# Ternary weights made on GpSimd alone, partly inside a self attention loop; a norm root moved; expert rows numbered by lane

## The reference, cut to what matters

```python
x = x + wkv(layernorm(x), ctx)                 # stage 0, a recurrence as scans
x = x + self_attention(layernorm(x))           # stage 1: 16 heads, one shared key/value per token,
                                               #          picked by the argmax of a gate
x = x + cross_attention(layernorm(x), ctx)     # stage 2: int8-rounded norm and weights
x = x + f8_matmul(layernorm(x))                # stage 3
x = x + channel_attention(layernorm(x), ctx)   # stage 4: softmax over channels, 128 units
x = x + ternary_ffn(layernorm(x))              # stage 5: weights as below
x = x + batch_attention(layernorm(x), ctx)     # stage 6
x = x + experts(layernorm(x))                  # stage 7: top 2 of 8 experts per token

def ternary_quant(w_fp32, g=64):
    w = w_fp32.astype(bfloat16); w_g = w.reshape(-1, g)
    scale = clip(mean(abs(w_g), -1), 1e-8, None)
    q = clip(round(w_g / scale), -1, 1)
    return w + ((q * scale).reshape(w.shape) - w)
```

## Time and profile before

| what | value |
|---|---|
| median of 3 runs | 828.03 us (826.43 to 833.64) |
| profiled execution, its own time | 824.63 us |
| its span, first to last instruction | 822.9 us |
| mean granted TensorE clock | 0.892 of full |
| busy: TensorE matmul, VectorE, ScalarE, GpSimd | 636.2, 502.4, 288.2, 247.4 us |

### The profile page before, as it was taken

One profiled execution on the slowest core, in us unless ns is written; L12 is line 12 of the kernel. 1 busy time (PEld: TensorE's weight loads), 2 busy tenths in 40 slices (PEclk: granted clock), 3 DMA queues, 4 the chain that ended last, 5 costly groups with the idle time before them and its releaser, 6 DMA issues.

```text
span 822.9 us, 10939 instructions
## 1 busy us (share of the span) xinstructions
PE 636.2 (77%) x3677; PEld 400.8 (49%) x3678; DVE 502.4 (61%) x1083; ACT 288.2 (35%) x519; POOL 247.4 (30%) x247
## 2 busy tenths in 40 slices
PE   1632888885972278889878999843999999999991
PEld 1331335443662124555544667531566666666661
DVE  6998986875988899999666445853222222222223
ACT  4810432324567005767843234501122111111210
POOL 3212243546821297644221015001111111111110
PEclk9885998997996559999979999955999999999996
DMA  7002302020005433561310003994000000000004
GB/s 256 0 0 55 112 1 65 14 52 0 2 1 104 98 83 96 139 167 52 92 39 1 0 1 150 430 427 143 20 26 26 25 25 25 25 25 25 19 14 166
DMA packets 34140, 61.83 MB, mean 75 GB/s; under 512 B 6232, under 2 KB 29784, under 8 KB 31768
## 3 DMA queue, kind: packets, MB, share of 16 engines
q1 hardware_dynamic: 24992, 48.93, 18.7%
q10 hardware_dynamic: 6896, 6.29, 2.3%
q0 software_dynamic: 2208, 6.03, 2.3%
HBM read 47.35 MB, written 13.50 MB: 74 GB/s over the span
## 4 chain that ended last, share of the span: by engine, by line
PE 47%; DVE 22%; DMA 3%; issue 3%; ACT 1%; POOL 1%; DVEq 0%; SPq 0%; POOLq 0%; ACTq 0%
PE bank L1820 17%; PE bank L1841 8%; DVE region L1191 4%; PE bank L1429 4%; PE bank L1450 3%; PE bank L1114 2%; DMA norm_rows<-XN 2%; PE bank L1831 2%; PE bank L1074 2%; PE bank L1098 2%; DVE XN L357 1%; DVE wide L1178 1%; PE bank L1955 1%; DVE region L1264 1%; DVE region L756 1%
## 5 line engine op out<-in xcount | busy, mean ns | idle before, releaser
L1820 PE MATMUL bank<-region,wide 128*128 x368 | 143.6, 544 | 0.3 <-issue 0.3
L1720 DVE TENSOR_TENSOR wide<-wide,bank 128x448 f32<-128x448 f32 x46 | 28.6, 621 | 127.3 <-ACT wide L1764 127.3
L1820 PEld LDWEIGHTS bank<-region,wide 128*128 128x128 f32 x368 | 68.8, 192 | 61.3 <-issue 61.1
L1191 DVE TENSOR_REDUCE region<-bank 128x2 f32<-128x512 f32 x128 | 80.3, 679 | 3.5 <-PE bank L1074 3.1
L1137 ACT ACTIVATE region<-bank 128x1024 f32<-128x1024 f32 x64 | 63.1, 1025 | 47.8 <-PE bank L1098 47.7
L1626 POOL DMA_INDIRECT choice_results<-wide,to_row x23 | 22.7, 987 | 181.6 <-DVE wide L1733 181.6
L1841 PE MATMUL bank<-region,XN 128*128 x322 | 73.4, 380 | 1.2 <-DVE wide L1733 1.2
L1074 PE MATMUL bank<-region 128*128 128x256 bf16 x256 | 53.2, 308 | 19.1 <-DVE region L1191 15.1
L1764 ACT ACTIVATE wide<-bank 128x448 f32<-128x448 f32 x46 | 25.0, 543 | 111.8 <-PE bank L1820 111.8
L1841 PEld LDWEIGHTS bank<-region,XN 128*128 128x128 f32 x322 | 59.6, 190 | 9.2 <-issue 2.1
L371 POOL TENSOR_TENSOR rstd<-vareps,half_neg 128x4 f32<-128x4 f32 x16 | 17.3, 1084 | 120.0 <-DVE vareps L367 119.8
(11 more groups left out here) (304 smaller groups left out, 1229.5 us busy)
## 6 DMA issues: line engine op xcount, KB each, us to landing
region<-in_L_ffn_experts_dram SPq DMA_DIRECT2D x8, 2688.0 KB, 24.0
region<-ctx_parts SPq DMA_DIRECT2D x24, 192.0 KB
region<-norm_parts SPq DMA_DIRECT2D x24, 192.0 KB
channel_values<-wide ACTq DMA_DIRECT2D x8, 512.0 KB, 4.4
ctx_parts<-region SPq DMA_DIRECT2D x40, 64.0 KB, 2.1
region<-in_L_ffn_w_gate_up_dram SPq DMA_DIRECT2D x4, 512.0 KB, 6.4
wide<-channel_values SPq DMA_DIRECT2D x16, 128.0 KB, 2.5
norm_parts<-region SPq DMA_DIRECT2D x24, 64.0 KB, 3.2
```

The lines of the kernel that those rows point to most:

```text
L1191: e.tensor_reduce(nmax[i % 2][:, at_:at_ + KC], score_bank("scores", n).rearrange("p (c n) -> p c n", c=KC), AX.X, ALU.max, negate=True).t ...
L1720: e.tensor_tensor(HB8[par][:, cols], silu8[:, cols], bank[hf][:, 512:512 + I8 // 2], ALU.mult)\
L1820: last = e.matmul(bank[hf][:, 512 * gu:512 * gu + hw], xbT[par][:, P * c:P * c + P], region[:, bass.ds(off + (2 * gu + c) * I8 + hw * hf, ...
```

## The change

1. VectorE's two compares per chunk are gone. GpSimd makes each chunk with six instructions: the quotient by the scale (to f32), two clamp-and-round steps (`tensor_scalar` with two operations each), times the scale, minus w, plus w. VectorE's closing step of the sums makes a reciprocal instead of two thresholds.
2. Nine of the 36 instructions run in the self attention loop, behind the context part of turns 2 to 8 (1, 1, 1, 2, 2, 1, 1 of them). The other 27 run in one row after GpSimd's splits of the norm in the channel attention, with no semaphore between them and VectorE.
3. At the start of the cross attention, the key blocks of tiles 0 and 1 and the norm root come ahead of the value bias of tiles 0 and 1.
4. The token row number becomes 8 * lane + tile. The norm rows are stored in two halves, each as soon as its half of the norm is there, with 4 KB pieces; results come back with 2 KB pieces. One VectorE instruction of the row search becomes two of half the width.

```diff
-        tscale, tlow, thigh = beside(TG), beside(TG), beside(TG)
+        tscale, tinv = beside(TG), beside(TG)
+        tsign = beside(1024, BF16)
+        EARLY6 = 9
...
@@ pool_attention, s == 0, turn t >= 1
                         for p in ((0,), (1, 2), (3,), (4,), (5,), (6, 7), (8,), (9,))[t - 1]:
                             pool_context_part(e, ch, p // 5, p % 5)
+                        if t == 2:
+                            e.wait_ge(s_tern["weights_summed"], 1)
+                        for p in ((), (0,), (1,), (2,), (3, 4), (5, 6), (7,), (8,))[t - 1]:
+                            pool_ternary_op(e, ch, p // 6, p % 6, traw[0])
@@ pool_attention, s == 1
+                for i in range(2):
+                    kbd(i)
+                pool_norm(e, 2, 4, NT)
+                e.wait_ge(s_att["norm_quantised"], NT)
                 for i in range(NT):
-                    kbd(i)
+                    if i >= 2:
+                        kbd(i)
                     e.tensor_tensor(V[:, i, :], V[:, i, :], bvrow, ALU.add).then_inc(s_att["v_ready"], 1)
                     e.wait_ge(s_att["v_ready"], i + 1)
-                    if i == 1:
-                        pool_norm(e, 2, 4, NT)
-                        e.wait_ge(s_att["norm_quantised"], NT)
@@ pool_channel_tiles
-            for c in range(TW // TCH):
-                pool_ternary_weights(e, ch, c)
+            for step in range(6 * TW // TCH):
+                if step // 6 * 6 + step % 6 >= EARLY6:
+                    pool_ternary_op(e, ch, step // 6, step % 6, f8a)
@@ vec_channel
-            pair_steps([(maxima, 0), (maxima_parts, 1), (weights, 0)])
+            pair_steps([(maxima, 0), (maxima_parts, 1)])
@@ vec_ternary_sums, last chunk
-                e.tensor_scalar(thigh, tscb, 0.5 + 2.0 ** -9, None, ALU.mult)
-                ch.link(e.tensor_scalar(tlow, tscb, -(0.5 + 2.0 ** -9), None, ALU.mult))
+                ch.link(e.reciprocal(tinv, tscb))
+                e.tensor_scalar(tinv, tinv, 0.5 / (0.5 + 2.0 ** -9), None, ALU.mult).then_inc(s_tern["weights_summed"], 1)
+        def pool_ternary_op(e, ch, c, step, tquot):
...
+                ch.link(e.tensor_tensor(by_group(tquot), by_group(w), spread(tinv[:, g]), ALU.mult))
+                ch.link(e.tensor_scalar(tquot, tquot, 1.0, MAGIC, ALU.min, ALU.add))
+                ch.link(e.tensor_scalar(tsign, tquot, MAGIC - 1.0, MAGIC, ALU.max, ALU.subtract))
+                ch.link(e.tensor_tensor(by_group(tsign), by_group(tsign), spread(tscb[:, g]), ALU.mult))
+                ch.link(e.tensor_tensor(tsign, tsign, w, ALU.subtract))
+                ch.link(e.tensor_tensor(w, w, tsign, ALU.add))
@@ results_in
-                            ys_dram[N * k + 2 * P * j:N * k + 2 * P * (j + 1), :].rearrange("(t p) d -> p t d", p=P))\
+                            ys_dram[N * k:N * k + N, :].rearrange("(p t) d -> p t d", t=NT)[:, 2 * j:2 * j + 2, :])\
@@ vec_experts
-            ch.link(e.tensor_scalar(hi_hot[:, :, 0, :], hi_hot[:, :, 0, :], lane_1, None, ALU.mult))
+            for k in range(2):
+                last = e.tensor_scalar(hi_hot[:, NT * k:NT * k + NT, 0, :], hi_hot[:, NT * k:NT * k + NT, 0, :],
+                                       lane_rows[:, k:k + 1], None, ALU.mult)
+            ch.link(last)
@@ act_experts
-            leave_half(XT8, 0, 6, s_turn, s_turned, base=TURN["moe"])
-            leave_half(XT8, 1, 0, s_turn, s_turned, base=TURN["moe"])
+            for hf in range(2):
+                e.wait_ge(s_xn, 7 * NT + 4 * (hf + 1))
+                e.dma_start(xn_dram.rearrange("(p t) d -> p t d", t=NT)[:, 4 * hf:4 * hf + 4, :],
+                            XN[:, 4 * D * hf:4 * D * hf + 4 * D].rearrange("p (t d) -> p t d", d=D))\
+                    .then_inc(s_moe["norm_stored"], 16)
+                leave_half(XT8, hf, (6, 0)[hf], s_turn, s_turned, base=TURN["moe"])
...
-            e.wait_ge(s_xn, 8 * NT)
-            e.dma_start(xn_dram.rearrange("(t p) d -> p t d", p=P), XN[:, :].rearrange("p (t d) -> p t d", d=D))\
-                .then_inc(s_moe["norm_stored"], 16)
```

42 lines of the change are left out of this document (14 added, 28 removed).

## The result

The kernel after took 822.32 us (median of 20 runs, 818.81 to 827.14), the kernel before 827.39 us (20 runs, 824.69 to 833.64). The ratio is 0.9936, 95% interval 0.992 to 0.9952: 5.1 us faster by the medians, about half of what was forecast, and within 1%. The two profiled executions have spans of 820.4 (after) and 822.9 us (before) and granted clocks of 0.884 and 0.892.

A forecast was written before the change was run, and what follows sets the result against it. VectorE was taken as the bound, busiest in the channel attention with TensorE close behind. Terms +0.1 + 6.2 - 1.6 - 11.5 - 2.8 - 0.3 = -9.9 us took 828.0 to 818.1 us, range 810.5 to 826.5.

The forecast's parts named there:

- channel attention: Compares leave VectorE, TensorE narrowly becomes the bound, last maxima end at 382.1 against 393.64: -11.5 us (-15 to -7).
- nine instructions in the loop: Self attention loop: GpSimd's added instructions delay key blocks and VectorE's select, +6.2 us (+3 to +11).
- norm root first: Start of cross attention: two bias additions leave GpSimd's list ahead of the norm root, -1.6 us (-1.8 to 0).
- store of the norm rows: Start of the experts: halves land by about 550, so `from_row` sets off the first fetch, -2.8 us (-2.9 to 0).
- results' return: End of the experts: 2 KB pieces may shorten the return of the results, -0.3 us (0 to -0.8).
- The rival that named it: GpSimd's `tensor_scalar` takes 2.13 or more; turns 3, 7 and 8 bring 2 to 4 us more: 821 us, chance 0.1.
- turns 7 and 8, +0.2: Self attention loop: each adds 1.04 us on GpSimd, last key blocks late by -0.5 to +1.0: +0.2 us.
- turn 3, put at 0: Self attention loop: adds 1.04 us on GpSimd, but the scores it feeds start later than GpSimd is done: 0.
- a rival with 0.07: Self attention loop: longer key-block waits drop TensorE's clock in five more turns, +15.8 on the sum, 834 us; chance 0.07.
- The steps by position: Self attention loop, costs worked along GpSimd's order: turn 2 +1.8, turns 3 and 4 0, turn 5 +1.15, turn 6 +3.0 us.
- The rival of late maxima: Channel attention stays bound by maxima queued behind operand loads; gain 6 in place of 11.5, 823.6 us; chance 0.15.
- 49 us, 57 at the upper bound: Channel attention: GpSimd's 27 late instructions run from 302 to 351 to 359, hidden, as TensorE wants the weights after 380.

The follow-up runs named there:

- before_rows: The kernel before with only the experts' part of the change (row numbering, halved norm-row store, 2 KB result pieces): 824.86 us, ratio 0.9957.
- nine_int16: The kernel after, early instructions kept in the loop, rounding by three (mult, add) `tensor_scalar` instead of two of 3.64 us: 816.84 us, ratio 0.9899.
- all_late: The kernel after with all 36 GpSimd instructions in the late row of the channel attention, none in the self attention loop: 823.77 us, ratio 0.9946.
- before_root_first: The kernel before with only the norm root of stage 2's second half moved ahead of the second value bias add: 827.33 us, ratio 1.001.
- late_int16: The kernel after with all ternary instructions late, clamp and round by three (mult, add) `tensor_scalar` through int16: 808.48 us; repeat 810.15 us.

## Why the prediction was right or wrong

By the time it was right in direction and range: 822.3 in 810.5 to 826.5. Its 818.1 lay 4.2 us too low: 9.9 us of gain were forecast and 5.1 measured. The range is 16 us wide, so lying in it says little, and the outcome that the prediction held likeliest, over 1% faster at 0.59, didn't come; within 1% had 0.36. It is also in part luck: the loop cost 6.7 us more than its term and the channel attention gave 2.6 more than its own, which partly cancel. (The range's lower end, worked out as the text says, is 818.1 - 3.2 - 2.5 = 812.4, not near 811.) Term by term, with what the traces gave; they add up to the 2.5 us between the two spans, not to the 5.1 of the medians:

| term | forecast | trace |
|---|---|---|
| closing step of the sums | +0.1 | at most +1.3 by the second key repeat; before_rows, without it, had +1.0 |
| nine instructions in the loop | +6.2 (+3 to +11) | +12.9 |
| norm root first | -1.6 | -1.7 local |
| channel attention | -11.5 (-7 to -15) | -14.1 |
| store of the norm rows | -2.8 | -3.4 |
| first expert block | none | +1.6, by the clock |
| results' return | -0.3 (-0.8 to 0) | +0.6 |

- **What failed is the sum of the loop**, +6.2 against +12.9, in two places of it. The first is the size "I take 1.04, since it reads one input as the cast does". The number of inputs doesn't set this price, the operations do: 3.64 us. It shows in "turns 7 and 8, +0.2", the tail: +5.1. The rival that named it had stopped at 2.13 and some 2 to 4 us. Removing it from the loop is worth 4.1 us in the profile (181.3 to 177.2) and 5.5 by the medians of after and nine_int16, though these were not run side by side.
- The second is turn 3, put at 0 and measured at 2.7: TensorE's longer wait in turn 2 and the clock behind it. I priced the waits as waits and kept the clock for a rival with 0.07, arguing from L524 at 0.39 behind a wait of 1.80. Behind 3.81 it was 0.61 and the clock 0.50. This rival happened in part: turns 2, 3 and 6 and the tail ran at 0.84 to 0.91 in the mean. It wasn't the five more turns that I priced at 15.8, so it didn't end slower than before. The Trainium skill, page TensorE: Matmul & The Clock Gate, Part 1, was cited for this, and the trace agrees with it: the throttled state is where TensorE falls back to. It doesn't account for all falls here: in turn 4 of the kernel before the clock was 0.73 in the mean, and in that turn and the one before it TensorE never stood longer than 1.4 us.
- **The steps by position held, and the contention with them.** The waits of 3 to 4 us at the scores of tiles 2 and 6 came as 3.81 and 4.57. Turn 2 cost 1.3 of 1.8, turn 5 1.2 of 1.15, turn 6 2.6 of 3.0, each by VectorE's select held up beside GpSimd's products, as the prediction says of L731. In turn 2 it is right in size by another way than its own: it reasoned from the delay of the key blocks, which TensorE pays in turn 3. Turn 4 cost 0, as forecast. With the fast form the loop cost 6.7 to 8.4, near the forecast 6.2, but partly by another cause, the clock.
- **The channel attention went as described**: TensorE became the bound at 2.85 us per two pairs. Its term was 2.6 us too small, mostly because six microseconds at half clock were allowed for the double work, which cost 3.0 us. The double work began at 314.20 and the clock was full from 315.8 on (0.78 in the mean from 314 to 318), so 1.6 us at half speed cost 0.8. The rival of late maxima can be laid aside: VectorE idled 4.4 us in all.
- "49 us, 57 at the upper bound" for the late row was 69.5: it began at 312.6, as the whole stage came 12 us later, and ended at 382.1. In all_late TensorE wanted the weights at 396.90 - 11.79 = 385.1, 3.9 us behind the last maxima; by the same distance it wants them at 395.7 in the kernel after. So the cover of over 20 us was 13.6, and nine instructions more would have used it up.
- **Store**: right in size and releaser. What the first block then lost (1.6 us) goes with the clock, as the windows at before_rows show. **Return**: wrong sign; 2 KB pieces took 5.05 us to the first landing (5.20 in before_rows), 1 KB pieces 4.46 (4.18 in before_root_first).

## What to carry to other kernels

An engine that is busy for 40% of a loop isn't free if it hands the loop on: price an instruction put there by the small instructions of VectorE that it holds up, by what waits for the one behind it, and then by the clock that TensorE comes back with; in this loop 1.9 us of GpSimd work cost some 3. Work with a far deadline belongs in a stage where nobody waits for its engine (in the middle of this kernel the same nine instructions cost 3.4 us instead of 10.3), and before moving it, look for a cheaper form: three instructions of 1.05 us took the place of two of 3.64, and the question of where to put them was gone.

## What the runs showed of the hardware

- GpSimd's `tensor_scalar` on 128 x 1024: (mult, add) 1.04 us; minimum, addition or product alone 2.8; (min, add) and (max, subtract) 3.64. So two operations can cost less than one. Output in f32, bf16 or int16, or int16 input, made no difference for (mult, add) (1.05 us each in late_int16). Its conversion to int16 clamps at the ends of the type: late_int16 has no other clamp, and its output is right.
- VectorE is held up by GpSimd's products with two inputs, until the product ends: L737 and L740 (128 x 16 values, 0.23 us otherwise) took 1.33 and 1.55 us and ended at 113.32 and 115.31, beside L1260 and L424, which ended at 113.28 and 115.28. VectorE's reduction L739 beside the same L424 took its usual 0.17. VectorE's L778 with two SBUF inputs took 1.39 us beside L424 (118.21 in the kernel before). Beside the 3.64 us `tensor_scalar` (130.99 to 134.63) the same instruction, now L784, took its usual 0.42:

```profile
130.99 3.64 POOL L1264 TENSOR_SCALAR region<-region 128x1024 bf16<-128x1024 f32 x1
...
133.29 0.42 DVE L784 TENSOR_TENSOR X<-X,region 128x256 f32<-128x256 f32 x1
```

  The Trainium skill, page GPSIMD Engine Reference, section 1 Specifications, names VectorE's side of this (two-port modes, two SBUF inputs). By these rows it also matters which instruction GpSimd runs: what its products with two inputs held up, its `tensor_scalar` with one didn't. No VectorE `tensor_scalar` was looked at beside the latter.
- A turn of the loop takes 9.35 us at full clock and some 12.2 to 12.5 in a turn where it falls, and in which turn that happens differs between executions of one kernel: late_int16 had one such turn of 12.5 us in its loop, its repeat two (12.2 and 12.5). That is 3 us a turn, and most of the spread of 8 us between runs of one kernel may be of this kind; it wasn't followed further.
